# Where the second attention's first exponentials start among the row maxima of its first three quads

## What is computed

```python
c_q = x @ W_dq
Q = (c_q @ W_uq).reshape(Bx, Sx, N_HEADS, D_K)
c_kv = x @ W_dkv
K = (c_kv @ W_uk).reshape(Bx, Sx, N_HEADS, D_K)
V = (c_kv @ W_uv).reshape(Bx, Sx, N_HEADS, D_K)
scores = jnp.einsum('bqhd,bkhd->bhqk', Q, K) / math.sqrt(D_K)
causal = jnp.tril(jnp.ones((Sx, Sx), dtype=bool))
scores = jnp.where(causal, scores, -jnp.inf)
attn = jax.nn.softmax(scores, axis=-1)
out = jnp.einsum('bhqk,bkhd->bqhd', attn, V).reshape(Bx, Sx, N_HEADS * D_K)
return out @ W_o
```

## Time and profile before

| | us |
|---|---|
| median of 3 runs (lowest, highest) | 1095.62 (1094.85, 1097.84) |
| the profiled execution, device time | 1096.86 |
| the profiled execution, span of the trace | 1095.1 |
| second attention, from the first maximum to the parts of quad 2's maxima | 593.9 to 680.1 |

### The profile page before, as it was taken

One profiled execution on the slowest core, in us unless ns is written; L12 is line 12 of the kernel. 1 busy time (PEld: TensorE's weight loads), 2 busy tenths in 40 slices (PEclk: granted clock), 3 DMA queues, 4 the chain that ended last, 5 costly groups with the idle time before them and its releaser, 6 DMA issues.

```text
span 1095.1 us, 17969 instructions
## 1 busy us (share of the span) xinstructions
PE 970.0 (89%) x6123; PEld 466.8 (43%) x6131; DVE 756.3 (69%) x1559; ACT 559.9 (51%) x618; POOL 346.8 (32%) x740
## 2 busy tenths in 40 slices
PE   6799999999999777799747889999999989999996
PEld 4222223322224444599624323333333335666664
DVE  6689999999987686244346967877777325654456
ACT  4479889888987322122215025555555774422232
POOL 2164345245345300578802013333333441000000
PEclk8599999999999999899965559999999999999999
DMA  5301101110200302277535231122111300001001
GB/s 189 105 1 44 45 1 43 43 30 13 82 1 17 115 29 53 66 177 182 83 86 196 82 101 29 61 90 89 45 44 45 103 2 1 1 15 44 1 1 39
DMA packets 49838, 65.45 MB, mean 60 GB/s; under 512 B 7801, under 2 KB 37849, under 8 KB 46297
## 3 DMA queue, kind: packets, MB, share of 16 engines
q1 hardware_dynamic: 44144, 60.21, 17.7%
q0 software_dynamic: 5632, 4.46, 2.8%
HBM read 51.74 MB, written 12.91 MB: 59 GB/s over the span
## 4 chain that ended last, share of the span: by engine, by line
PE 62%; DVE 23%; issue 7%; ACT 4%; DMA 1%; POOL 1%; SPq 1%; DVEq 0%; ACTq 0%; POOLq 0%
PE causal_ps L1218 9%; PE acc_ps L765 9%; PE acc_ps L1093 6%; DVE mx L516 6%; PE tail_ps L1039 5%; PE tail_ps L1233 5%; DVE R L1569 4%; PE causal_ps L1076 4%; DVE tails L1575 3%; PE causal_ps L964 3%; PE causal_ps L727 2%; PE tail_ps L964 2%; PE acc_ps L974 2%; PE causal_ps L738 2%; ACT EX L1436 2%
## 5 line engine op out<-in xcount | busy, mean ns | idle before, releaser
L1436 ACT ACTIVATE EX<-causal_ps 128x1024 f32<-128x1024 f32 (+1 forms) x160 | 147.2, 939 | 159.8 <-PE causal_ps L1076 158.6
L516 DVE TENSOR_REDUCE mx<-tail_ps 128x1 f32<-128x512 f32 x266 | 157.7, 633 | 41.2 <-PE tail_ps L1042 22.7
L1310 ACT ACTIVATE R<-R 128x2048 f32<-128x2048 f32 (+1 forms) x80 | 134.7, 1737 | 0.5 <-DVE R L1569 0.5
L1218 PE MATMUL causal_ps<-XT,w 128*128 128x512 f32 x256 | 115.7, 594 | 1.0 <-DVE hid_f L1994 1.0
L1076 PE MATMUL causal_ps<-QE,KE 75*128 75x512 bf16 (+3 forms) x384 | 103.9, 342 | 10.9 <-ACT EX L1436 5.7
L1039 PE MATMUL tail_ps<-KM,QM 72*128 72x512 bf16 (+1 forms) x320 | 105.2, 357 | 8.7 <-DVE mx L516 3.0
L1569 DVE TENSOR_SCALAR R<-causal_ps 128x1024 f32<-128x1024 f32 (+1 forms) x88 | 94.1, 1071 | 15.2 <-PE causal_ps L727 14.1
L2217 POOL TENSOR_TENSOR pacer<-eps_ln 128x1 f32<-128x1 f32 x160 | 31.5, 197 | 226.7 <-ACT EX L1436 226.0
L1317 ACT ACTIVATE R<-R 128x1792 f32<-128x1792 f32 (+4 forms) x80 | 100.5, 1268 | 0.0
L1575 DVE TENSOR_REDUCE tails<-causal_ps 128x1 f32<-128x768 f32 (+4 forms) x96 | 93.0, 968 | 10.6 <-PE causal_ps L738 9.8
L1477 ACT ACTIVATE act_f<-causal_ps 128x512 f32<-128x512 f32 x64 | 38.2, 598 | 119.2 <-PE causal_ps L1218 119.2
(11 more groups left out here) (297 smaller groups left out, 1615.6 us busy)
## 6 DMA issues: line engine op xcount, KB each, us to landing
QS<-q_parts SPq DMA_DIRECT2D x8, 576.0 KB
KS<-k_parts SPq DMA_DIRECT2D x24, 192.0 KB
QM<-q_parts SPq DMA_DIRECT2D x8, 576.0 KB
KM<-k_parts SPq DMA_DIRECT2D x24, 192.0 KB
QE<-q_parts SPq DMA_DIRECT2D x8, 576.0 KB
KE<-k_parts SPq DMA_DIRECT2D x24, 192.0 KB
wg<-in_wg_t SPq DMA_DIRECT2D x16, 256.0 KB
wu<-in_wu_t SPq DMA_DIRECT2D x16, 256.0 KB
```

The lines of the kernel that those rows point to most:

```text
L516: return reduce(mx[:, par, hh, o0:o0 + step * (cnt - 1) + 1:step], scores[:, 0:cnt * w].rearrange("p (c w) -> p c w", w=w), AX.X, op, **how)
L1218: mm = pe.matmul(banks[2 * m + o], w[:, k, m * P:(m + 1) * P], XT[:, n * BANK:(n + 1) * BANK], start=True, stop=True)
L1310: act.activation(R4[:, rp, h0:h0 + 2, 0:width], R1[:, rp, h0:h0 + 2, 0:width], ACT.Square).then_inc(squared, 1)
L1436: act.activation(EX[:, rp, hh, 0:width], causal_ps[hh % 2][:, 0:width], ACT.Exp, scale=float(D) ** -0.5).then_inc(exp_done, 1)
```

## The change

Only the order of work and the place of some tiles in PSUM changes; nothing is added or left out of the computation. BEFORE_EXP = 14 of quad 1's 40 maxima stay ahead of the exponentials, and the other 26 go to tail_ps, two of them ahead and 24 among the steps 0 and 1 of quad 0's exponentials (11 and 13). The 40 maxima of quad 2, so far at the steps 1 to 4 of that quad, stand at its steps 2 to 4 (14, 13, 13). DVE does the parts of quad 0's maxima straight after the 40th maximum, and PE's transposition stands 5 jobs into quad 1. The parts of quad 1's maxima are turned after the third matmul of step 2, into tail_ps. SP loads QE and KE of quad 0 at once, stores and reloads the maxima of quad 0, and only then loads QM and KM of quad 2 and QE and KE of quad 1. The quads 1 to 7 of the exponentials keep their order.

```diff
-FIRST_TURN = 8
+FIRST_TURN = 5
+BEFORE_EXP = 14
+SECOND_AT = [BEFORE_EXP, BEFORE_EXP + 13, len(MAX), len(MAX), len(MAX), len(MAX)]
+THIRD_AT = [0, 0, 0, 14, 27, len(MAX)]
...
-            for par in range(2):
-                sp.wait_ge(first_full, len(MAX) * (par + 1))
-                load_max(2 + par, par)
-                store_max(par)
-                load_exp(par, par)
+            load_exp_stack(0, 0)
+            store_max(0)
+            load_exp_rows(0, 0)
+            load_max(2, 0)
+            load_exp_stack(1, 1)
+            sp.wait_ge(first_full, len(MAX) * 2)
+            load_max(3, 1)
+            store_max(1)
+            load_exp_rows(1, 1)
...
+            def second_job(n):
+
+                pe.wait_ge(first_max, len(MAX) + n - 1)
+                row_scores(tail_ps[:, n % 2 * BANK:(n % 2 + 1) * BANK], 1, n).then_inc(first_full, 1)
...
-                for i in range(len(MAX)):
+                for i in range(BEFORE_EXP if g else len(MAX)):
                     first_job(g, i)
-
-            pe.wait_ge(first_max, 2 * len(MAX))
+            for n in range(2):
+                second_job(BEFORE_EXP + n)
+            pe.wait_ge(first_max, len(MAX) + BEFORE_EXP)
...
+            def first_exp_quad():
+
+                pe.wait_ge(exp_in[0], 16 * (STACK_DMAS + 1))
+                for s in range(NS):
+                    jobs = [cut for hh in range(HQ) for cut in exp_scores(0, 0, s, hh)]
+                    if s:
+                        jobs = jobs[:2] + spread(jobs[2:], exp_sums(0, 0, s - 1))
+                    second = [(0, lambda n=n: second_job(n)) for n in range(max(SECOND_AT[s], BEFORE_EXP + 2), SECOND_AT[s + 1])]
+                    third = [(0, lambda n=n: max_job(2, 0, n)) for n in range(THIRD_AT[s], THIRD_AT[s + 1])]
+                    if s == 2:
+                        run_all(jobs[:3])
+                        turn_max(1)
+                        pe.wait_ge(max_in[0], 16 * STACK_DMAS * 2)
+                        jobs = jobs[3:]
+                    run_all(among(jobs, second + third))
...
-                src = (acc_ps if isinstance(g, int) and g < 2 else tail_ps)[0:HQ * KT, 0:P]
+                src = (acc_ps if isinstance(g, int) and g == 0 else tail_ps)[0:HQ * KT, 0:P]
...
-                maxima(g, n, banks[i % 6], dve.tensor_reduce, ALU.max, negate=True).then_inc(first_max, 1)
-                if i == len(MAX) + FIRST_TURN - 1:
+                bank = 4 + n % 2 if i >= len(MAX) + BEFORE_EXP else i % 6
+                maxima(g, n, banks[bank], dve.tensor_reduce, ALU.max, negate=True).then_inc(first_max, 1)
+                if i == len(MAX) - 1:
                     parts_of_max(0, 0)
```

More of the change, by code:

```diff
@@ L630, in store_max, with load_exp_stack, load_exp_rows @@
                 sp.dma_start(one_of_rows(m_rows, g).rearrange("r (h t) -> h r t", t=P), mparts[:, :, :]).then_inc(m_out, 16)
-            def load_exp(g, par):
+            def load_exp_stack(g, par):
+                load_stack(QE[:, par, :, :], KE[:, par, :, :], g, exp_in[par])
+            def load_exp_rows(g, par):
                 sp.wait_ge(m_out, 16 * (g + 1))
-                load_stack(QE[:, par, :, :], KE[:, par, :, :], g, exp_in[par])
                 sp.dma_start(QE[ROWS:MROWS, par, :, :].rearrange("r h t -> r (h t)"), one_of_rows(m_rows, g)
@@ L655, in _ @@
                     sp.wait_ge(exp_summed, NS * (2 * j + 1 + par))
-                    load_exp(2 * j + 2 + par, par)
+                    load_exp_stack(2 * j + 2 + par, par)
+                    load_exp_rows(2 * j + 2 + par, par)
             for par in range(2):
@@ L659, in _ @@
                 sp.wait_ge(exp_summed, NS * (NQ - 3 + par))
-                load_exp(NQ - 2 + par, par)
+                load_exp_stack(NQ - 2 + par, par)
+                load_exp_rows(NQ - 2 + par, par)
             sp.wait_ge(max_full, len(MAX) * (NQ - 2))
@@ L1142, in project_first, with exp_quad @@
                     times_w(1, n, 5)
-            def exp_quad(g, k, par, with_max, first=False, turn_maxima=True, beside=None):
+            def first_exp_quad():
[12 more added lines that the diff above has]
+                    run_all(among(jobs, second + third))
+            def exp_quad(g, k, par, with_max, turn_maxima=True, beside=None):
                 pe.wait_ge(exp_in[par], 16 * (STACK_DMAS + 1) * (k + 1))
@@ L1150, in exp_quad @@
                     run_all(exp_scores(g, par, 0, hh))
[L1151 to L1158, removed]
-                run_all(exp_scores(g, par, 0, 2))
[L1160 to L1167, removed]
+                if turn_maxima:
+                    turn_max(g + 1)
+                run_all(exp_sums(g - 1, 1 - par, NS - 1))
+                run_all(exp_scores(g, par, 0, 2))
+                pe.wait_ge(m_sb, g + 2 if turn_maxima else NQ)
+                at_least(pe, e_normed, g - 1)
+                if not turn_maxima:
+                    pe.wait_ge(yt_sb, CH + CH // B)
+                    pe.wait_ge(z_sb, CH + CH // B)
+                turn_exp(g - 1)
                 run_all(exp_scores(g, par, 0, 3))
@@ L1173, in exp_quad @@
                             among(jobs, beside[s]) if beside else jobs)
-            exp_quad(0, 0, 0, True, first=True)
+            first_exp_quad()
             exp_quad(1, 0, 1, True)
```

## The result

The changed kernel is 0.6% slower, where a gain was forecast.

The account below looks back on a forecast made before the run. DVE's row maxima were taken to bound the stretch ahead of the exponentials. Starting these 14.6 us earlier, less work added in steps 0 to 4, left 4.0 us: 1091.6 us from a median of 1095.62, range 1087.5 to 1096.5.

Parts of the forecast that it names:

- What is taken away at the front: Before quad 0's exponentials: 26 maxima fewer stand ahead, so they start 14.6 us earlier, at 625.4; store 1.5 us.
- What is put on at steps 0 and 1: Quad 0: 24 added maxima make PE the bound, 21.8 us at half clock plus waits; step 1 ends at 645.5.
- neither count that gave the rise of the clock: Steps 0 and 1: clock rises at 638 by PE's gapless time, or at 643 by the first group of sums.
- the saving of 2.2 us: Steps 0 and 1: gain taken for the clock's rise before step 1 ends, from between 4.1 and 2.0 us.
- The new wait: Step 2 of quad 0: PE waits around the transposition of quad 1's maxima; 3.3 us from its last maximum to quad 2's.
- The start of the exponentials: Quad 0: first exponentials at 625.4 in place of 639.97, 14.6 us earlier.
- the term of steps 2 to 4: Quad 0: 40 maxima at about 0.6 us and 2.6 us of sums, taken as 26.7 us, ends 24.6 and 29.4.
- the low clock: Rival: half clock stays through steps 2 to 4 of quad 0, 8 us later, 1103.5 us; chance 0.05.
- quads 1 to 7 have the same jobs at the same clock, and what follows is shifted as a whole: After quad 0: nothing is reordered, so the 4.0 us gained by the parts of quad 2's maxima carries to the end.
- the three things that were to show it wrong: DVE idle over 4 us in steps 2 to 4, the clock falling again there, or the start slipping for the maxima's rows.
- The second sign: Steps 2 to 4 of quad 0: DVE standing idle for more than 4 us would show the prediction wrong.
- PE, even at 1.2 GHz, waits for it: Stretches 593.9 to 615.9 and 622.3 to 639.9: DVE's row maxima set the pace and PE waits, even at half clock.

Follow-up runs that it names:

- step 2 filled: Changed kernel with nine unused matmuls in PE's two waits in step 2 of quad 0: 1091.81 us, ratio 0.9975 to the kernel before.
- the changed kernel with the delay: Changed kernel with eight unused matmuls at the start of quad 1, so all that follows comes 1.0 us later: 1096.24 us, ratio 1.0011 to the kernel before.

## Why the prediction was wrong

**Right.** *What is taken away at the front*: the parts (22.2 us, forecast 22.1), the store (1.5 us), no wait for the rows, nothing lost on SP. *What is put on at steps 0 and 1*: first exponential scores to last maximum of quad 1 took 20.2 us (625.25 to 645.47) against 20.1 forecast. That is in part luck: neither count that gave the rise of the clock held. It came after 17.7 us without a gap on PE (12.5 before) and 3.5 us behind the first group of sums (7.3 before). From the first exponential scores these counts put it at 12.6 and 17.6 us; it came at 17.7, at the late end, and the saving of 2.2 us that I took was that of the late end. *The new wait*: 3.5 us against 3.3.

**Mis-sized.** The start of the exponentials was earlier by 12.9 us, not 14.6. The sum counted 14 maxima of 0.55 us behind the parts; the order that I had quoted has a 17th job ahead of the first exponential scores, and it waits for the 15th maximum, whose own scores had waited 1.98 us for the 13th. That is 1.7 us. Moving the scores ahead of it won 1.0 us back and nothing in the end.

**The step that failed first** is the term of steps 2 to 4, 26.7 us, which took 30.8. The pace of 0.6 us for a maximum and 2.6 us for the sums was near the truth: with the clock held it was 27.9, inside the ends of 24.6 and 29.4. What failed was the price of the wait in front of it. I charged it with its 3.3 us and nothing else, and gave the low clock a chance of 0.05 because "quad 1 has just such gaps". It has not. In its stretch PE idles 1.2 us in 29.4; here it idled 2.3 us out of about 3.5, less than 4 us after the clock had risen. The condition I named for that rival, a low spell of 14 us beyond 649, was not needed: 10.2 us cost 2.9 (30.8 against 27.9), the 0.3 us for each that I had given, and that alone was most of the 4.0 us gain. In the profile where it lasted 23.9 us, parts of quad 1 to parts of quad 2 took 38.2 us against 30.6 with step 2 filled, 7.6 us more, again 0.3 for each.

**The step that failed worst** is "quads 1 to 7 have the same jobs at the same clock, and what follows is shifted as a whole". It cost 4.9 us in the profile. A shift was taken for harmless, but it is not: in the profiled executions a quad at whose start the clock falls takes 37.5 us in place of 34.8, and 0.3 us in the moment of the start, counted from the clock's last rise, parted a quad with a fall from one without. I could not have worked out the place. But the waits of about 1.0 and 0.5 us at the start of nearly every quad were in the trace of before, just outside the stretch that I had read (685.4 to 714.8), and the range held nothing for them.

**The sum of the misses**: 1.8 us at the front, 4.1 in steps 2 to 4, 0.1 between them, 4.9 in quads 1 to 5 and 0.7 behind, 11.6 us from the first maximum on. The median missed by 11.2, but not by this sum alone: 1.2 of it is that the median before, 1095.62 of 3 runs, was 1096.84 over 20.

**Its own signs.** Two of the three things that were to show it wrong came: the clock fell in steps 2 to 4, and DVE stood idle there for 7.1 us. The second sign was set too low, for with the clock held DVE still idled 4.4 us.

**Slips in the working.** "PE, even at 1.2 GHz, waits for it" isn't in the rows for the first stretch, where PE is busy 22.00 of 22.00 us; it fits the second, 14.80 of 17.60. And 0.4 us for each microsecond from 638 and 643 to 647.7 gives 3.9 and 1.9, not 4.1 and 2.0. No term hangs on either by more than 0.2 us.

The Trainium skill, page "TensorE: Matmul & The Clock Gate", section "A second HAM failure mode: psum-queue depth-cycling", tells of a clock that swings because a queue that goes through PSUM banks idles PE in small pieces. I set it against a row of clock 1.00 and gave it little. The trace agrees with it as to small idle pieces: 0.63 and 1.69 us in step 2, 1.04 and 0.48 us at a quad's start, were each followed by a fall. The banks alone don't do it: with the same two banks and the same order, but the two waits filled, the clock stayed at 1.00 from 643.6 to 885.9.

**Still open.** The runs show that whether the clock falls at a quad's start hangs on its moment; by what rule, they don't show. Nor is it shown why the clock in quad 0 rose at 643 in one execution and 649.6 in another, or stayed low until 674 in one, nor why step 2's low spell lasted 10.2 us in two profiles and 23.9 in a third. The spread of the runs (1090 to 1096 for step 2 filled, 1094.9 to 1110.3 for the changed kernel with the delay) goes with each run's mean granted clock: with step 2 filled the eight runs up to 1092.72 had 0.934, the four from 1095.01 on 0.931. Which spells make the difference, one profile a kernel can't show. That a late start of quad 1 also saves the changed kernel is read from the runs' times and mean clocks; no profile shows those falls gone.

## What to carry to other kernels

A wait on PE has two prices, its length and what the clock does behind it; where a change puts a new wait of a microsecond or two into a dense stretch, fill it with matmuls whose result nobody reads, and cost it again without the clock's share before judging the change itself. Where a loop has equal short waits that the clock survives just so, a shift of a few tenths of a microsecond can be worth 2 or 3 us, so a small difference between two orders says little about the orders: compare both with the waits filled. And when two orders of the same work differ in when they start an engine, sum the binding engine's busy time over the whole stretch first; here it left 1 or 2 us to be had, not 14.

## What the runs showed of the hardware

Unexpected were three things. Nine unused matmuls, some 1.9 us of PE work, made the changed kernel 10.0 us faster (1101.83 to 1091.81), and five others, at the start of quad 1, brought back 3.7 us of that by the ratios and 7 by the medians, with intervals that overlap a little. A low spell of 6.8 us in a quad cost 2.6 to 2.7 us (37.4 and 37.5 against 34.8 and 34.9), nearly the 3.4 us (an estimate, half of 6.8) that the half clock would cost a fully busy PE. And in the front PE ran at 0.50 for 22 us while it was busy without a gap (22.00 of 22.00 us), on score matmuls of 72 rows and weight loads between them. In the changed kernel with its front filled that stretch was the same (20.83 of 21.00 us at 0.50), but behind it, with four unused matmuls of 128 rows and 512 columns from 615.15 on and one behind each further job, the clock rose at 619.5, 24 us earlier from the first maximum than in the changed kernel.
